# Per-sequence order of an attention and feed-forward kernel: output projection ahead of the first layer, second layer with its weights held still

## What is computed

```python
q, k, v = (einsum('blh,dh->bdl', u, W) + b for each of three W, b)
k  = causal_conv(k, k_kernel) + k_D * k          # FFT in the reference
kv = k * v
y  = (causal_conv(kv, ssm_kernel) + kv * D) * q
x  = layernorm(u + einsum('blh,oh->blo', y, Wo) + bo)
h  = square(relu(x @ W_fc.T))                    # 256 -> 1024
y2 = h @ W_proj.T                                # 1024 -> 256
n  = spikes of a five-step neuron driven by y2   # 0..5, a staircase of y2
out = layernorm(x + n / 5)
```

## Time and profile before

| | |
|---|---|
| runs before, median of 3 | 1035.83 us (1032.44 to 1038.37) |
| the profiled execution's own time | 1035.66 us |
| its span in the profile | 1033.7 us |
| mean granted TensorE clock | 0.896 |
| PE, DVE, ACT, POOL busy, share of the span | 77%, 74%, 56%, 40% |

### The profile page before, as it was taken

How to read it: one execution, slowest core, us unless ns; L and a number is a source line. 1 busy time by engine, 2 the same in 40 slices (tenths; PEclk the granted TensorE clock), 3 DMA queues, 4 the chain that set the end, 5 groups by cost and what they waited for, 6 DMA issues and landing times.

```text
span 1033.7 us, 27885 instructions
## 1 busy us (share of the span) xinstructions
PE 792.9 (77%) x12032; PEld 649.8 (63%) x12032; DVE 770.1 (74%) x1087; ACT 579.9 (56%) x560; POOL 414.9 (40%) x306
## 2 busy tenths in 40 slices
PE   0178878777678787856499888898888988889983
PEld 0178877777678786846356566565666655666652
DVE  7986868685748666866658877887778887778884
ACT  3489767676747667631345535554445554455551
POOL 0273222222212222211445446654466544565542
PEclk9989989898788889867589989998999999899997
DMA  9838888888777888898100111101111001110001
GB/s 348 285 83 209 204 212 209 207 207 204 172 203 172 219 182 224 185 210 219 34 1 1 42 41 41 41 0 41 41 41 41 9 32 41 41 41 31 10 21 41
DMA packets 39292, 118.35 MB, mean 114 GB/s; under 512 B 3872, under 2 KB 23200, under 8 KB 31008
## 3 DMA queue, kind: packets, MB, share of 16 engines
q1 hardware_dynamic: 37824, 114.71, 42.6%
q10 hardware_dynamic: 1376, 2.23, 0.6%
HBM read 106.69 MB, written 27.01 MB: 129 GB/s over the span
## 4 chain that ended last, share of the span: by engine, by line
issue 25%; PE 20%; POOL 19%; DMA 17%; DVE 15%; ACT 3%; POOLq 0%; SPq 0%; DVEq 0%; ACTq 0%
DMA arena<-kpad_dram 15%; PE ps L667 11%; POOL arena L593 10%; PE ps L645 6%; POOL arena L600 2%; DVE arena L1045 2%; POOL arena L582 2%; DVE arena L953 2%; PE ps L761 2%; DVE arena L1064 2%; DVE arena L936 2%; POOL arena L587 2%; POOL arena L597 1%; PE ps L725 1%; ACT arena L465 1%
## 5 line engine op out<-in xcount | busy, mean ns | idle before, releaser
L667 PE MATMUL ps<-arena 128*128 128x64 f16 (+3 forms) x6144 | 193.6, 188 | 78.4 <-issue 44.3
L593 POOL TENSOR_TENSOR arena<-arena 128x512 f16<-128x512 f32 x128 | 165.8, 1316 | 197.7 <-ACT arena L481 194.0
L667 PEld LDWEIGHTS ps<-arena 128*128 128x128 f16 x6144 | 188.5, 102 | 82.2 <-issue 77.8
L429 ACT ACTIVATE arena<-arena 64x3584 f16<-64x3584 f16 x60 | 188.4, 3181 | 63.5 <-DVE arena L936 63.4
L645 PE MATMUL ps<-arena 128*128 128x96 f16 x3072 | 149.0, 213 | 78.0 <-DVE arena L898 54.7
L768 PE MATMUL ps<-arena 128*128 128x256 f16 x1536 | 192.4, 287 | 8.7 <-POOL arena L593 6.2
L552 POOL TENSOR_TENSOR arena<-arena 128x512 f16<-128x512 f32 x32 | 84.9, 2653 | 272.6 <-ACT arena L423 272.6
L645 PEld LDWEIGHTS ps<-arena 128*128 128x128 f16 x3072 | 143.3, 102 | 80.8 <-issue 67.1
L768 PEld LDWEIGHTS ps<-arena 128*128 128x128 f16 x1536 | 157.4, 104 | 41.8 <-POOL arena L593 10.8
L936 DVE TENSOR_TENSOR arena<-arena 64x512 f16<-64x512 f16 x128 | 104.9, 834 | 95.8 <-DMA arena<-kpad_dram 95.7
L761 PE MATMUL ps<-arena 128*128 128x512 f16 x768 | 170.0, 382 | 2.5 <-DVE arena L1071 2.5
(11 more groups left out here) (91 smaller groups left out, 726.4 us busy)
## 6 DMA issues: line engine op xcount, KB each, us to landing
arena<-kpad_dram SPq DMA_DIRECT2D x128, 512.0 KB, 6.7
kpad_dram<-ksplit_dram SPq DMA_DIRECT2D x16, 1024.0 KB, 9.9
qy<-in_uT SPq DMA_DIRECT2D x8, 1024.0 KB, 17.3
arena<-in_u SPq DMA_DIRECT2D x16, 512.0 KB, 4.2
out<-arena SPq DMA_DIRECT2D x16, 512.0 KB, 3.1
arena<-in_k SPq DMA_DIRECT2D x2, 512.0 KB, 4.8
ksplit_dram<-arena ACTq DMA_DIRECT2D x2, 512.0 KB, 3.6
arena<-in_wfT SPq DMA_DIRECT2D x1, 1024.0 KB, 10.8
```

What stands on the lines that cost most here:

```text
L429: nc.scalar.activation(*shifted(windows_of(0, s, half)), ACT.Copy).then_inc(c1_copied, 1)
L593: nc.gpsimd.tensor_tensor(h16[:, 1, f], h_square[:, f % 4], h16[:, 0, f], ALU.subtract).then_inc(h_lo, 1)
L667: last = nc.tensor.matmul(out[:, ch * COL + delta * B:(ch + 1) * COL], win[:, delta * P:(delta + 1) * P], data(xp, ch)[:, 0:cols], start=( ...
```

## The change

It moves project_out(i+1) from behind up(i) to ahead of it, and turn_y from the next sequence to the one after it, behind up(i). In the second layer the weights are now the stationary operand and 512 tokens move: 48 products of 512 columns, whose result has channels on the partitions. The spike counts (bfloat16) are therefore turned back by eight products with a bfloat16 identity (`turn_counts`, between parts 3 and 4 of the next sequence's up), and second_sum reads them from PSUM (PN, in the banks of PT). down_done is now signalled after each half of the channels. On DVE first_sum(i+1) goes ahead of the squares, second_sum(i-1) behind square 4, and norm_shift(0) behind square 6. On ACT norm(1, i-1) goes behind x_turn(i+1). On POOL root(0) comes after h_part 3, root(1) after h_part 7, and gather runs one sequence further ahead, behind add_bo.

```diff
 ACT
-            def body(i, r, first, last, turn=None):
-
-                if not first and not last:
-                    y_turn(i + 1)
+            def body(i, r, left, turn=None):
+                first = isinstance(i, int) and i == 0
                 if not first:
                     act.wait_ge(down_done, i * 2)
...
+                if left > 1:
+                    y_turn(i + 2)
+                if left:
+                    if not first:
+                        act.wait_ge(sum2_ready, i)
+                    norm(0, i + 1, 1 - r)
+                    x_turn(i + 1, 1 - r)
                 if not first:
                     if turn is not None:
 
                         act.wait_ge(stored[1 - r], 16 * turn)
                     norm(1, i - 1, 1 - r)
-                if not last:
-                    norm(0, i + 1, 1 - r)
-                    x_turn(i + 1, 1 - r)
 POOL
                 for f in range(FT):
                     h_part(i, f)
-                    if f == 4 and not first:
-                        root(1, i - 1)
-                if left:
-                    root(0, i + 1)
+                    if f == ROOT_AFTER and left:
+                        root(0, i + 1)
+                if not first:
+                    root(1, i - 1)
                 if left > 1:
-                    gather(i + 2, r)
                     add_bo(i + 2, r, nth)
-
-            body(0, 0, 2, 2, True)
+                if left > 2:
+                    gather(i + 3, 1 - r)
 PE
+            def down_part(t, f, h, w, first, last):
+
+                return nc.tensor.matmul(PD[:, t], wp16[:, w, f, t * P:(t + 1) * P], h16[:, h, f], start=first, stop=last)
...
+            def turn_counts(i):
+                pe.wait_ge(stair, i * STAIRS + STAIRS)
+                for j in range(NI):
+                    for t in range(DT):
+                        last = nc.tensor.matmul(PN[:, j, t * P:(t + 1) * P], spike_count[:, t * L + j * P:t * L + (j + 1) * P],
+                                                ident16[:, :], start=True, stop=True)
+                last.then_inc(counts_turned, 1)
+
+            def body(i, r, left):
+                if left:
                     project_out(i + 1)
+                up(i, r, range(0, 4))
+                if not (isinstance(i, int) and i == 0):
+                    turn_counts(i - 1)
+                up(i, r, range(4, FT))
+                if left > 1:
+                    turn_y(i + 2, r)
                 down_first(i)
-                down(i, 1)
-                if not last:
-                    turn_x(i + 1, 1 - r)
-                down(i, 3)
+                down_second(0)
+                if left:
+                    turn_x(i + 1, 1 - r, left > 1)
+                down_second(1)
 DVE
+                if not last:
+                    first_sum(i + 1, 1 - r)
                 for f in range(FT):
                     square(i, f)
-                    if f == 2 and not first:
+                    if f == 4 and not first:
                         second_sum(i - 1, 1 - r, isinstance(i, int) and i == 1)
+                    if f == 6 and not last:
+                        norm_shift(0, i + 1)
                 if not first:
                     norm_shift(1, i - 1)
-                if not last:
-                    first_sum(i + 1, 1 - r)
-                spikes(i, 0, range(0, 3))
+                spikes(i, 0, range(0, len(theta)))
                 if not last:
                     split_x(i + 1, 1 - r)
-                spikes(i, 0, range(3, len(theta)))
                 spikes(i, 1, range(0, len(theta)))
```

More of the change, by code:

```diff
@@ L32 @@
 UP = TOK // NU
+ROOT_AFTER = 3
 EPS = 1e-5
@@ L513, in _ @@
             x_turn(0, 0)
[L514 to L520, removed]
+            body(0, 0, 2)
+            body(1, 1, 2)
+            body(2, 0, 2)
+            with act.Fori(1, B // 2 - 2) as pair:
+                body(pair * 2 + 1, 1, 2, pair)
+                body(pair * 2 + 2, 0, 2, pair)
+            body(B - 3, 1, 2, B // 2 - 2)
+            body(B - 2, 0, 1, B // 2 - 2)
+            body(B - 1, 1, 0, B // 2 - 1)
             act.wait_ge(stored[1], 16 * (B // 2 - 1))
@@ L578, in gather @@
             def gather(i, r):
-                if not isinstance(i, int):
+                if not isinstance(i, int) or i >= 2:
                     pool.wait_ge(y_turned, i - 1)
@@ L609, in _ @@
             add_bo(1, 1, 1)
+            gather(2, 0)
             def body(i, r, nth, left, first=False):
@@ L744, in project_out, with turn_x, up @@
                 last.then_inc(wo_done, 1)
-            def turn_x(i, r):
+            def turn_x(i, r, y_before=True):
                 pe.wait_ge(x1_ready, i + 1)
-                if isinstance(i, int) and i == 0:
-                    pe.wait_ge(yT_ready, 2)
+                if y_before:
+                    pe.wait_ge(yT_ready, i + 2)
                 turn(x1[:, r], x_turned)
-            def up(i, r):
+            def up(i, r, parts):
                 pe.wait_ge(x_hi, i + 1)
                 pe.wait_ge(x_lo, i + 1)
-                for f in range(FT):
+                for f in parts:
                     if not (isinstance(i, int) and i == 0 and f < 2):
@@ L776, in down_first @@
                     pe.wait_ge(h_hi, i * FT + f + 1)
-                    for j in (0, 2):
-                        for w in range(2):
-                            down_part(i, j, f, 0, w, f == 0 and w == 0, False)
+                    for w in range(2):
+                        down_part(0, f, 0, w, f == 0 and w == 0, False)
                 for f in range(FT):
                     pe.wait_ge(h_lo, i * FT + f + 1)
-                    for j in (0, 2):
-                        down_part(i, j, f, 1, 0, False, f == FT - 1)
@@ L785, in down, with down_second @@
-            def down(i, j):
-                for f in range(FT):
+                    last = down_part(0, f, 1, 0, False, f == FT - 1)
+                last.then_inc(down_done, 1)
+            def down_second(part):
+                for f in range(FT // 2 * part, FT // 2 * (part + 1)):
                     for h, w in ((0, 0), (0, 1), (1, 0)):
-                        last = down_part(i, j, f, h, w, f == 0 and (h, w) == (0, 0), f == FT - 1 and h == 1)
-                last.then_inc(down_done, 1)
@@ L791, in body @@
[L791 to L794, removed]
-                if not last:
-                    project_out(i + 1)
-                down_first(i)
-                down(i, 1)
-                if not last:
-                    turn_x(i + 1, 1 - r)
-                down(i, 3)
-            pe.wait_ge(id_done, 1)
+                        last = down_part(1, f, h, w, f == 0 and (h, w) == (0, 0), f == FT - 1 and h == 1)
@@ new lines, in down_second @@
+                if part:
+                    last.then_inc(down_done, 1)
+            def turn_counts(i):
[5 more added lines that the diff above has]
+                last.then_inc(counts_turned, 1)
@@ L810, in _ @@
             pe.wait_ge(f_hi, 2)
[L811 to L815, removed]
+            body(0, 0, 2)
+            with pe.Fori(0, B // 2 - 2) as pair:
+                body(pair * 2 + 1, 1, 2)
+                body(pair * 2 + 2, 0, 2)
+            body(B - 3, 1, 2)
+            body(B - 2, 0, 1)
+            body(B - 1, 1, 0)
+            turn_counts(B - 1)
         @block.vector
```

32 lines of the change are left out of this document (18 added, 14 removed).

## The result

| | before | changed |
|---|---|---|
| median of 4 runs | 1037.1 us (1032.44 to 1040.91) | 1049.15 us (1045.45 to 1054.03) |
| profiled execution, its span | 1035.66, 1033.7 us | 1047.61, 1045.8 us |
| PE, DVE, ACT, POOL busy | 77%, 74%, 56%, 40% | 76%, 69%, 55%, 40% |
| mean granted TensorE clock | 0.896 | 0.903 |

The change makes the kernel slower by 1.26% (ratio 1.0126, 95% interval 1.0083 to 1.0169), 12 us in the profiled pair. 1066 us was forecast, 30 us more than before. (A fourth run of the kernel before stands beside the three of the first table, which moves its median from 1035.83 to 1037.1.)

What follows compares the result with a forecast made beforehand. The late load holding first_sum, then squares beside POOL, was to bound the kernel: 17.4 + 13.3 + 0.7 + 2.2, plus 0.7 for the clock, a 34.3 us period. 1035.66 + 0.2 - 2.2 + 13 x (34.3 - 31.84) gave 1066 us, range 1036 to 1085.

Steps and rivals of the forecast that it cites:

- The wait: On DVE ahead of first_sum: it waits for POOL's add_bo and the late load of u, idling over 4 us.
- from the first square to the next D: DVE's squares and what stands among them, 13.3 us; then the high half, 0.7, and ten PE products, 2.2.
- D: End of the first 24 products of a sequence's second layer on PE, from which the prediction counts.
- The chain from D to the first square: turn_x, x_turn, norm(1), store and load of u, add_bo, first_sum and moments: 17.4 us.
- Its low bound: Squares lose little to POOL and the clock stays full: period 31.7 to 32.2 us, total 1032 to 1038.
- The clock: PE's ten products before D cost up to 2.2 us more at the lower clock; a third, 0.7, was taken.
- break-even: Period of the changed kernel at which it would equal the kernel before: 32.0 us.
- The ends: Outside the 13 periods: D of sequence 1 0.2 us later; from D of sequence 14 to the end 2.2 sooner.
- the likeliest case: The load wait lengthens the period to 33 to 35.8 us: total 1049 to 1085, chance 0.70.
- The faster rival: The load doesn't delay first_sum; POOL's low halves bind, period 29.3 to 31.4 us, total 1001 to 1028; chance 0.11.
- The rival of an earlier clock fall: PE's clock falls inside up, slowing up, turn_y and down_first: period 36 to 37 us, 1087 to 1100; chance 0.08.
- the saving of 0.5 us: On PE's second layer: 48 products of 512 columns take 10.4 us instead of 10.9.

Runs made afterwards that it cites:

- the early load: Changed kernel with SP issuing the load of u ahead of the store that waits for norm(1): 1005.94 us, ratio 0.9716.
- the longer chain: Changed kernel with POOL's gather put between the arrival of u and add_bo: 1060.36 us, ratio 1.0271.
- the two kernels that realise it: Changed kernel with u loaded ahead of SP's store, 1005.94 us; the same with add_bo also waiting for norm_shift(1), 994.64 us.
- ACT's order: Changed kernel with only norm(1, i-1) put back ahead of norm(0, i+1) on ACT: 1048.53 us, ratio 1.0099.

## Why the prediction was right or wrong

**The mechanism** was right, the size was not: 30 us were forecast and 12 measured. The wait, its place, its releaser and its 13 times are as written, and the runs with the early load and with the longer chain show it on the path. The step that failed is the term "from the first square to the next D", put at 13.3 us for the squares and what stands among them.

**The chain from D to the first square** was forecast at 17.4 us and measured 17.2 (768.4 to 785.59). The wait itself, "over 4 us", is 4.2.

**From the first square to the last** is the term that was mis-sized: forecast 13.3, measured 11.9 (785.59 to 797.50, and 11.91 or 11.92 in all of the 12 middle sequences). I had squares alternate with POOL whenever both had work, at 1.56 us. Square 7, behind norm_shift, took 0.68 and not 1.56, which is 0.9 of the 1.4 us; squares 5 and 6 took 2.2 and not 2.56, another 0.4. The first five came out right by luck, at 5.1 where 5.0 was forecast: squares 0 to 3 took 2.46 us in a row, with POOL's first L602 made to wait, but square 4 waited 1.12 us for the first low half, which I had left out. The prediction's own row had 6.47 us for five squares, 1.3 each. Its low bound had 11.5. That makes the period at full clock 32.0 us instead of 33.6.

**The clock** was forecast at a third of 2.2 us, 0.7. It fell in 5 of 12 sequences and cost 1.7 us there (6.61 against 4.92), 0.7 on the mean, and in sequence 14 as well. The size was right, but by luck: the rows before could not show in how many sequences. It decides the result: at full clock the period is 32.0 us, which is the prediction's break-even, so the loss of 12 us is about what the clock's falls cost, 6 times 1.7 to 2 us.

**The ends.** D of sequence 1 came at about 572.5, forecast 573.0, before 572.84. In sequence 14 the comparisons start at 1000.37, so 13 periods took 427.8 us, 32.9 each, where 34.3 was forecast. From there to the end of the span it is 45.5, forecast 44.7, before 46.9. Together -0.3 - 1.4 + 13 x 1.07 = 12.2, the measured 12.1 us of the spans (1045.8 - 1033.7). Of the forecast's 30 us, 18 were the 1.4 us of the squares, 13 times. (The terms that the prediction lists behind D of sequence 14 add up to 44.3 and not 44.7, which changes nothing.)

**The rivals.** The time of 1049.15 is at the lower edge of the likeliest case. The faster rival, no wait for the load, was put at 1001 to 1028; the two kernels that realise it gave 1006 and 995, the second below that range, and add_bo does hold norm_shift (2.30 us). A period of 29.3 to 31.4 was forecast for it; 29.3 was measured in most sequences with norm_shift held, so the 2 us did not add up as the rival had it, and 29.04 without. The rival of an earlier clock fall did not occur in the middle sequences of the changed kernel, but did with the longer chain, inside up. The period there was still 34.0 us, the 32.0 of full clock and the 2.0 added to the chain.

**The products.** 24 of 512 columns stayed at 0.22 us each, turn_counts took 0.61 us and not 1.0; alone they changed nothing, as argued. But the saving of 0.5 us that the prediction reads from its rows is not there. Its 0.113 us for one product of 256 columns comes from a row of 24 in 2.78 us, and such a row also holds the last product's own end, which is longer than the distance from one product to the next. These rows of the kernel before differ by 34 products and 3.71 us, 0.109 each:

```profile
755.78 5.18 PE L768 MATMUL ps<-arena 128*128 128x256 f16 x46
...
1002.17 1.47 PE L768 MATMUL ps<-arena 128*128 128x256 f16 x12
```

In the same way 24 products of 512 columns in 5.34 us and 12 in 2.75 give 0.216 each. So 96 old products take 10.47 us and 48 new ones 10.36, a saving of 0.11 us. The prediction's other figure, 0.12, was the right one; neither entered its sum.

## What to carry to other kernels

When a consumer moves ahead by half a period, look up what issues its input, not only how long the input takes: here the load stood in SP's queue behind a store whose condition had moved the other way in the same change. Undoing one part of such a change can be as slow as leaving it (ACT's order), while repairing the queue turned a loss of 1.3% into a gain of 2.8%, and of 4% with add_bo held back as well. And where two engines hold each other up, do not put every instruction at the price of full alternation: here a square that stood behind an instruction which had already waited took 0.68 us and not 1.56, and that alone was 0.9 us a period.

## What the runs showed of the hardware that was not expected

The same pattern of pauses on PE (0.9 us, two products, 1.03 us) brought the lower clock in 5 middle sequences of 12 and not in the others of one execution. In the kernel with the longer chain a pause of 3.3 us inside up, at about the same place in every sequence, made the following 12 products slower (4.1 to 5.3 us against 2.75), and the clock was at its upper level again for the burst that mattered. That slow stretch did not lengthen the period, while one in the burst right before the first signal lengthened it by 1.8 us.

DVE's second_sum shows what a source in PSUM is worth beside POOL. With both sources in SBUF, in the kernel before with norm(1) moved, it took 2.17 us beside POOL's low halves; in the changed kernel, with one source in PSUM, it took 1.21 us beside them (790.66, above):

```profile
754.61 2.17 DVE L1096 SCALAR_TENSOR_TENSOR arena<-arena 128x1024 f32<-128x1024 bf16 x1
```
